# Node sums that start from a copy of x: an adding scatter and a one-load layernorm chunk in a graph-network kernel

## What is computed

```python
def _edge_conv(x, src, dst, edge_attr, W, b, denom):
    msg = jnp.concatenate([x[src], edge_attr], axis=1) @ W + b
    s = jax.ops.segment_sum(msg, dst, num_segments=x.shape[0])
    return s / denom[:, None]          # denom = max(edges that end in the node, 1)

h = _edge_conv(x, ...W0)               # 128 features
outputs = [h]
for W, b in ((W1, b1), (W2, b2), (W3, b3)):
    outputs.append(_edge_conv(concatenate(outputs), ...W, b))
x = _layernorm(x + outputs[-1])        # eps 1e-5, no scale, no shift
```

## Time and profile before

| | |
|---|---|
| median of three runs | 1350.82 us |
| span of the profiled execution | 1364.5 us |
| busy | VectorE 767.9, GpSimd 804.8, TensorE 564.7, ScalarE 444.6 us |
| DMA | 265.36 MB, 194 GB/s over the span |
| preparation, products, round 1 | 0 to 405, 405 to 658, 658 to 781 us |
| list stage 1, round 2 | 781 to 985, 985 to 1104 us |
| list stage 2, round 3, rest | 1104 to 1148, 1148 to 1262, 1262 to 1364 us |

### The profile page before, as it was taken

One profiled execution on the slowest core, in us unless ns is written; L12 is line 12 of the kernel. 1 busy time (PEld: TensorE's weight loads), 2 busy tenths in 40 slices (PEclk: granted clock), 3 DMA queues, 4 the chain that ended last, 5 costly groups with the idle time before them and its releaser, 6 DMA issues.

```text
span 1364.5 us, 15423 instructions
## 1 busy us (share of the span) xinstructions
PE 564.7 (41%) x3008; PEld 422.7 (31%) x3020; DVE 767.9 (56%) x2933; ACT 444.6 (33%) x1066; POOL 804.8 (59%) x766
## 2 busy tenths in 40 slices
PE   2444525667757667766355300000045421565000
PEld 1444413445544333333354300000045411554000
DVE  7786777577773523323587654112277675776630
ACT  7543422333332333333144133000034431343530
POOL 5886643556634456656677356666477702775376
PEclk9666656666557888888667655555577765757555
DMA  2564469954105577777777478665666759664411
GB/s 58 192 225 143 122 200 364 358 193 146 42 15 185 192 241 251 248 242 247 243 254 250 140 231 270 174 194 166 177 223 235 268 161 301 221 255 137 126 51 38
DMA packets 157594, 265.36 MB, mean 194 GB/s; under 512 B 22672, under 2 KB 91367, under 8 KB 157472
## 3 DMA queue, kind: packets, MB, share of 16 engines
q1 hardware_dynamic: 112128, 149.57, 32.6%
q0 software_dynamic: 26240, 59.55, 15.8%
q10 hardware_dynamic: 19104, 54.92, 10.8%
HBM read 114.39 MB, written 149.75 MB: 194 GB/s over the span
## 4 chain that ended last, share of the span: by engine, by line
DVE 31%; issue 17%; PE 15%; DMA 12%; POOL 10%; SPq 6%; another core or an unknown queue 4%; ACT 2%; DVEq 2%; POOLq 0%; ACTq 0%
DVE stat L1379 4%; POOL out_rows L716 4%; SPq L444 4%; PE hp L1725 3%; DVE area L1394 3%; DVE area L1130 3%; PE segp L1725 2%; DVE area L1204 2%; PE segp L1767 2%; DMA SX<-part_rows,nlo 2%; POOL G L674 2%; DVE UT L1432 2%; PE hp L1767 1%; POOL G L682 1%
## 5 line engine op out<-in xcount | busy, mean ns | idle before, releaser
L639 POOL DMA_INDIRECT G<-x_in,srci x196 | 224.1, 1143 | 141.2 <-PE segp L1637 65.0
L654 POOL DMA_INDIRECT z_of_nodes<-area,sum_rows x144 | 142.3, 988 | 110.1 <-issue 52.4
L869 ACT ACTIVATE area<-area,shift,rs 128x128 f32<-128x128 f32 x390 | 153.2, 479 | 17.6 <-DVE shift L1401 16.2
L1761 PE MATMUL segp<-ZERO 128*128 128x384 f16 (+1 forms) x54 | 21.9, 405 | 320.8 <-DVE EC L1415 278.3
L862 ACT ACTIVATE sd<-dev,eps 128x13 f32<-128x13 f32 x30 | 9.2, 306 | 414.4 <-DVE dev L1387 376.5
L682 POOL DMA_INDIRECT G<-part_rows,s0r x70 | 77.7, 1110 | 81.2 <-DMA part_rows<-UT 55.7
L1761 PEld LDWEIGHTS segp<-ZERO 128*128 128x128 f16 x54 | 5.9, 110 | 324.7 <-DVE EC L1415 308.5
L1767 PE MATMUL segp<-G,EC 128*128 128x128 f32 (+1 forms) x432 | 80.5, 346 | 55.2 <-DMA G<-h_rows,dsti 22.5
L682 POOL DMA_INDIRECT G<-part_rows,previ x70 | 78.7, 1125 | 38.7 <-issue 19.8
L682 POOL DMA_INDIRECT G<-h_rows,dsti x70 | 78.5, 1122 | 33.1 <-issue 21.4
L844 ACT ACTIVATE area<-segp,zero,inv 128x512 f32<-128x512 f32 x72 | 54.7, 776 | 129.6 <-PE segp L1725 63.4
(11 more groups left out here) (398 smaller groups left out, 1547.4 us busy)
## 6 DMA issues: line engine op xcount, KB each, us to landing
part_rows<-area SPq DMA_DIRECT2D x36, 1024.0 KB
z_of_nodes<-ZERO ACTq DMA_DIRECT2D x28, 1024.0 KB
area<-x_in SPq DMA_DIRECT2D x30, 832.0 KB
area<-z_of_nodes SPq DMA_DIRECT2D x30, 832.0 KB
out_rows<-area ACTq DMA_DIRECT2D x30, 832.0 KB
part_rows<-ZERO SPq DMA_DIRECT2D x56, 256.0 KB
h_rows<-area SPq DMA_DIRECT2D x36, 258.0 KB
part_rows<-UT SPq DMA_DIRECT2D x60, 128.0 KB
```

Source lines behind the costliest of these rows:

```text
L639: g.indirect_dma_start(G[:, slot, 0:D], None, x, bass.IndirectOffsetOnAxis(ap=srci[:, c:c + 1].bitcast(u32), axis=0), bounds_check=last_no ...
L654: g.indirect_dma_start(ZF, bass.IndirectOffsetOnAxis(ap=sum_rows[:, c:c + 1], axis=0), HS3[:, b, j, 3 * D + 1:4 * D + 1], None, bounds_che ...
L869: last = a.activation(XL[:, b, k], XL[:, b, k], ACT.Identity, bias=shift[:, b, r:r + 1], scale=rs[:, b, r:r + 1])
```

## The change

The change has four parts. ZF rows 0 to 49999 are filled with a copy of x by 25 copies from one memory tensor to the other (2000 rows each, 80 runs of 12.8 KB), and one store of zeros fills the padding rows; they stand where the stores of zeros stood, so that the last two of the 28 places issue nothing. The scatter of line 654 adds to what the row holds (`compute_op=ALU.add`). A chunk is one load from ZF, without the VectorE addition, and the same for the last 80 rows. The ring has four buffers, the second tile is gone, and the load of chunk c + 2 stands at the place of chunk c, where it waits for the store of chunk c - 2.

```diff
-RING = 3
-ZRING = 2
+RING = 4
+AHEAD = 2
+XPIECES, XRUN = 25, 25
...
-        zfill = ZF.rearrange("(g p q r) c -> g p q (r c)", p=P, q=ZROWS // CG, r=CG)
+        pieces = lambda t: t[0:N, :].rearrange("(g a r) c -> g a (r c)", g=XPIECES, r=XRUN)
+        xcopy, zcopy = pieces(x), pieces(ZF)
+        zpad = ZF[N:N + ZROWS * P, :].rearrange("(p q r) c -> p q (r c)", p=P, r=CG)
...
-            e.dma_start(RX[0:LREST, 0, :], x[N - LREST:N, :]).then_inc(s["rest_in"], 16)
-
...
-            e.dma_start(RZ[0:LREST, :], ZF[N - LREST:N, :]).then_inc(s["rest_in"], 16)
+            e.dma_start(RX[0:LREST, 0, :], ZF[N - LREST:N, :]).then_inc(s["rest_in"], 16)
...
                 b = c % RING
                 if c >= RING:
                     e.wait_ge(st_o[b], 16 * (c // RING))
-                e.dma_start(XL[:, b, :], xv[c]).then_inc(ld_xz[b], 16)
-                if c >= ZRING:
-                    e.wait_ge(s["ln_stat"], c - ZRING + 1)
-                e.dma_start(ZL[:, c % ZRING, :], zv[c]).then_inc(ld_xz[b], 16)
+                e.dma_start(XL[:, b, :], zv[c]).then_inc(ld_xz[b], 16)
 
             def chunk(c):
-                if 1 <= c < LCH - 1:
-                    load_chunk(c + 1)
+                if 1 <= c < LCH - AHEAD:
+                    load_chunk(c + AHEAD)
...
-            load_chunk(0)
-            load_chunk(1)
+            for c in range(AHEAD + 1):
+                load_chunk(c)
...
-            e.wait_ge(s["cleared"], 32 * IT)
+            e.wait_ge(s["cleared"], 16 * (XPIECES + 1))
...
-                                                 bounds_check=last_sum, oob_is_err=False).then_inc(scat[b], 16)
+                                                 bounds_check=last_sum, compute_op=ALU.add).then_inc(scat[b], 16)
...
             def clear_sums(u):
                 for q in (0, 1):
-                    e.dma_start(zfill[2 * clear_at.index(u) + q], ZERO[:, :].unsqueeze(1).to_broadcast([P, ZROWS // CG, CW])).then_inc(s["cleared"], 16)
+                    g = 2 * clear_at.index(u) + q
+                    if g < XPIECES:
+                        e.dma_start(zcopy[g], xcopy[g]).then_inc(s["cleared"], 16)
+                    elif g == XPIECES:
+                        e.dma_start(zpad, ZERO[:, :].unsqueeze(1).to_broadcast([P, ZROWS // CG, CW])).then_inc(s["cleared"], 16)
...
             def stats_chunk(c):
                 b = c % RING
-                e.wait_ge(ld_xz[b], 32 * (c // RING + 1))
-                lnk(v.tensor_tensor(XL[:, b, :], XL[:, b, :], ZL[:, c % ZRING, :], ALU.add))
+                e.wait_ge(ld_xz[b], 16 * (c // RING + 1))
                 row_stats(b, LR, al, XL[:, b, :]).then_inc(s["ln_stat"], 1)
...
             q = slice(0, LREST)
-            e.wait_ge(s["rest_in"], 32)
-            lnk(v.tensor_tensor(RX[q, 0, :], RX[q, 0, :], RZ[q, :], ALU.add))
+            e.wait_ge(s["rest_in"], 16)
```

More of the change, by code:

```diff
@@ L206, in gnn_kernel @@
         rs = sb("rs", [P, RING, LR], f32)
-        RZ = sb("RZ", [P, D], f32)
         AREA = 8584
@@ L272, in gnn_kernel @@
         XL = carve([RING, LR * D], f32, 4)
-        ZL = carve([ZRING, LR * D], f32, 4)
         stat_l = carve([2, LB, 6], f32, 4)
@@ L339, in gnn_kernel @@
         LN_ROWS = LCH * SPAN
-        xv = x[0:LN_ROWS, :].rearrange("(g p r) c -> g p (r c)", p=P, r=LR)
         zv = ZF[0:LN_ROWS, :].rearrange("(g p r) c -> g p (r c)", p=P, r=LR)
-        zfill = ZF.rearrange("(g p q r) c -> g p q (r c)", p=P, q=ZROWS // CG, r=CG)
+        pieces = lambda t: t[0:N, :].rearrange("(g a r) c -> g a (r c)", g=XPIECES, r=XRUN)
+        xcopy, zcopy = pieces(x), pieces(ZF)
+        zpad = ZF[N:N + ZROWS * P, :].rearrange("(p q r) c -> p q (r c)", p=P, r=CG)
         ov = out[0:LN_ROWS, :].rearrange("(g p r) c -> g p (r c)", p=P, r=LR)
@@ L730, in _ @@
             for b in range(RING):
-                e.wait_ge(st_o[b], 16 * (LCH // RING))
+                e.wait_ge(st_o[b], 16 * len(range(b, LCH, RING)))
             e.wait_ge(s["rest_out"], 16)
```

## The result

The kernel after takes 1384.02 us (median of four runs, 1382.94 to 1388.88), the kernel before in the same comparison 1351.24 us: ratio 1.0261, interval 1.0226 to 1.0296. The change costs about 33 us. The forecast was a gain of 14 us; what came is rival A, a longer product stage, and the time lies near A's 1375 us.

A forecast was written before the change was run, and what follows sets the result against it. No engine was taken to bound the kernel, which goes stage by stage. Chunks -37, landing +18 and copy +5 gave -14 us: a profile of 1350.5 us, a median of 1337 us, range 1305 to 1395.

The forecast's parts named there:

- rival A: Product stage: the adding scatter lengthens it by more than the chunks give back; 1375 us, slower, chance 0.27.
- so I take no change: Issue of the adding scatter on GpSimd: same cost as plain; upper end 0.5 us each, up to +72 us.
- The landing, +18 us: Product stage: an adding scatter lands 1.0 us later, and 18 waits of VectorE show it; upper end +45 us.
- Theory L: Product stage, named after the profile: the adding scatter lands later and the loop waits for that, the forecast's +18 us.
- The chunks, -37 us: Rounds and list stages: gain from dropping 30 VectorE additions and half the chunk loads; bounds -15 to -56.6 us.
- Rival D: Rounds and list stages: the chunk work was mostly hidden, gaining only 16 us; sum +7, 1358 us, chance 0.12.
- list stage 2: Stage where VectorE works alone with the DMA: -7 us, from two additions of 3.8 us and less load traffic.
- The copy, +5 us: Preparation: six pieces of the copy, each 0.8 us dearer than zeros, delay the edge features; between -1 and +10 us.
- rival C: Preparation: slow copies cost +10 us at the edge features and some 6 us earlier; 1348 us, chance 0.10.
- The wait for the copies at the first scatter: First scatter: the wait for the fill stays covered, 100 us after its last issue; uncovered, a few us.
- Read-modify-write in flight together: Product stage: rows of an adding scatter do not queue for each other, so landing stays near the lower end.
- Ring of four, 0: Chunk loads: the fourth buffer and earlier load were given no gain of their own, 0 us.

The follow-up runs named there:

- m_mix: Measurement only: the four scatters of a group are plain with 128 rows, adding with 128, plain with 64, adding with 64; 1289.52 us in one profile.
- r_before: The kernel before, run again without any edit on a chip where before takes 1313.14 us; 1311.27 us, ratio 0.9976.
- e_add_only: The kernel before with only the scatter changed to the adding form, which adds to zeros; 1362.82 us, ratio 1.0362.
- e_copy_only: The kernel before with the copy of x in place of the zeros, scatter and chunks unchanged; 1320.78 us, ratio 1.0061.
- v_psum: The kernel before with ScalarE copying each chunk of sums to four PSUM banks, so VectorE's addition has one SBUF input; 1387.25 us, ratio 1.0165.
- v_psum4: v_psum with ScalarE's copy moved ahead of the previous chunk's normalisation, four buffers for x and one tile for the sums; 1280.71 us, ratio 0.9750.

## Why the prediction was wrong

**The step that failed** is "so I take no change", for the issue of an adding scatter on GpSimd. It rested on plain transfers of either direction, which all took 0.98 to 1.00 us. It measured +0.57 us, above even the upper end of 0.5. The reason given for that end (three descriptions for a row instead of two) does not fit either: m_mix shows nearly the same price for half the rows. 144 x 0.57 = 82 us of busy time came in; 44 us of GpSimd's idle time (110.1 to 65.8 us) absorbed part of it on record, 34 us on the chip of r_before; 36 to 48 us show. Rival A had named the place and the point from which it decides, 0.10 us a scatter, which was passed five times over. GpSimd's share of a step, 10.3 of 13.4 us, had been read correctly; 8 x 0.57 = 4.6 us more does not fit in the 3.1 us that were left. The lesson of the sum is that a slack of 3.1 us for 8 instructions, 0.39 us each, should have been set beside the upper end of 0.5 us, and then the chance of A was too low at 0.27.

A's place and mechanism came true. That its 1375 us lie so near the 1384 is partly luck: it had put 56 us on the stage, where 36 came on record, and 37 us on the chunks, where 24 came. It had also put 18 of the 56 us down to the landing. Against the forecast the spans on record are off by 31 us: 18 in the product stage and 13 in the stages of the chunks.

**The landing, +18 us.** The last scatter lands 3.3 us after its start instead of 2.5, +0.8 where I took +1.0. But 0.57 of it is the longer issue, and in the medians of e_add_only and e_copy_only it is all of it (0.56 us). No trace shows the 1.0 us of its own at which I had priced the read. Nor is the landing what shows: VectorE and ScalarE wait 307 us for landings and the stage is still GpSimd's 267.9 us of issue plus 8. Theory L would have left GpSimd idle; it is the one engine that is not. They wait because the scatters are issued later.

**The chunks, -37 us.** Right in size where it could be tested alone: -39, -39 and -40 us (0.9692, 0.9695, 0.9689), and by stages -13.4, -6.8, -11.7 and -6.8 against -13, -8, -12 and -4. Rival D, 16 us, falls. On record it was -24 us, since round 1 gave 4 us instead of 13; why stays open. The division was partly wrong: I had put waits for VectorE first and a quarter of the long gathers down to traffic. Of the 5.5 and 4.5 us of waits that I halved in rounds 2 and 3, moreover, 3.5 and 4.3 stand as "remote" in the earlier trace rows, with no work of this core named as their end. And list stage 2 was to give 7 us, of which 3.8 came on record and 5.0 on the other chip. The long gathers went altogether, and v_psum shows the reason: the addition with both inputs in SBUF. In order of time in the profile of before, an addition and the gather beside it:

```profile
750.38 1.94 DVE L1394 TENSOR_TENSOR area<-area 128x1664 f32<-128x1664 f32 x1
...
751.70 1.49 POOL L682 DMA_INDIRECT G<-h_rows,dsti  x1 [0.30 <-issue]
```

The addition ends at 752.32, the gather 0.87 us later. Of the 30 additions 27 lie beside a long gather (23 in the rounds, 4 in list stage 1), and each of these gathers ends 0.87 or 0.88 us after its addition. The Trainium skill ("SBUF — State Buffer", "Who interferes with whom") states this: a VectorE instruction with two inputs in SBUF contends with a GpSimd instruction that reads SBUF, through a shared read interface. This case's traces agree, 1.12 us for a gather with such additions, 1.00 to 1.01 us without them (after) and with one input in PSUM (v_psum). I had not drawn on it, and it would have made the chunk term surer, not the sign.

**The copy, +5 us.** +5.5 us on record, 6 us between the means elsewhere, inside the range given. The size is right by luck: I had priced a piece at 3.6 us of all engines against 2.8 for a store of zeros, and both take 2.9. The edge features come later all the same. One difference in the traces is that a piece of the copy goes in 16 packets of 64000 B, each of which keeps an engine for 2.9 us, and a store of zeros in 512 packets of 2048 B of 0.09 us. Whether the loads of the features wait behind the long packets was not tested, so the cause stays open. The estimate of 4.9 us for a piece and +13 us, from the Trainium skill's figure ("DMA: Bandwidth & Descriptors", "Latency and other measured facts"), lies above what these traces show. The sign for rival C, over 15 us of wait for the edge features, appeared (21.6 us) without C: on other chips before itself waits 13.6 to 15.0 us there, and v_psum4, with stores of zeros, 19.1, and of the 17 us more on record 12 come back before the first scatter. The wait for the copies at the first scatter did not appear, as said.

**Read-modify-write in flight together.** The rule of the Trainium skill that I cited ("DMA: Bandwidth & Descriptors", "Two DMAs through the same engine are not ordered") gives landings near the lower end; this case agrees with it, since the landing behind the issue grew by 0.2 us in the last scatter and by nothing in the medians. It says nothing of the issue, and I let it speak for the whole scatter.

**Ring of four, 0.** Right: 1325.81 against 1325.53 us.

## What to carry to other kernels

An instruction in a form that the trace doesn't contain has no price; where the engine that issues it has little slack per instruction, compare that slack with the upper end of the price before the forecast gets a sign. Work taken off VectorE can be paid for on GpSimd's queue, and a change with 40 us of gain and 47 us of loss looks like a small change from outside: ask for each part alone. An addition with both inputs in SBUF beside a stream of indirect gathers stretches them; one input in PSUM keeps the addition and frees the gathers, if the copy into PSUM stands early in its queue.

## What the runs showed that I had not expected

- An adding scatter holds GpSimd for 1.55 us where a plain one takes 0.985 us, and it moves its 128 rows as 128 packets instead of 16; with 64 rows it is 1.43 against 0.95 us. Its landing behind the issue took no longer in the medians of e_add_only and e_copy_only.
- A long gather ended 0.87 or 0.88 us after the two-input addition during which it started; 27 of 30 additions met one. With one input in PSUM the longest of 47 gathers beside an addition took 1.00 us.
- A copy from one memory tensor to the other in 64000 B packets kept the 16 engines for 2.9 us per MB, the same as a store of zeros in 2048 B packets, and the first scatter still came 6 us later.
- The same kernel takes 1307 to 1314 us on some chips and 1351 to 1361 us on others, and only traces of the latter have "remote" waits (VectorE 54.7 us in that of before). The cause is open.
